# A two-layer attention and mixture-of-experts kernel: start-up order, clearing of the experts' buffer, where the padding of an expert's tiles lies, and the unit at which small work is done

## The reference, cut to what matters

```python
# x: (64, 64, 256), context: (64, 64, 256), float32
x = x + L0_xattn(layernorm(x), ctx)   # 8 heads of 8 channels, rotary, out projection
x = x + L0_ffn(layernorm(x))          # 64 experts, top 8 of a softmax, no capacity limit
x = x + L1_xattn(layernorm(x), ctx)   # 8 heads of 8, no rotary, no out projection
x = x + L1_ffn(layernorm(x))          # 64 experts, top 8, at most 128 rows for each expert
# attention: q, k, v projections (C = 64 channels, T = 256 positions, per batch),
#            softmax(q k / sqrt(8)) v
# expert:    (silu(x Wg) * (x Wu)) Wd, Wg and Wu 256 x 96, Wd 96 x 256, weighted and summed
```

## Time and profile before

| what | us |
|---|---|
| median of three runs | 2247.05 |
| the three runs | 2241.72 to 2247.66 |
| the profiled execution | 2246.79 |
| its span, first to last instruction | 2245.0 |

### The profile page before, as it was taken

How to read it: one execution, slowest core, us unless ns; L and a number is a source line. 1 busy time by engine, 2 the same in 40 slices (tenths; PEclk the granted TensorE clock), 3 DMA queues, 4 the chain that set the end, 5 groups by cost and what they waited for, 6 DMA issues and landing times. The chain is left out here.

```text
span 2245.0 us, 45332 instructions
## 1 busy us (share of the span) xinstructions
PE 1681.1 (75%) x12724; PEld 1129.2 (50%) x12879; DVE 1462.2 (65%) x4525; ACT 1329.7 (59%) x3396; POOL 985.9 (44%) x1111
## 2 busy tenths in 40 slices
PE   1688888889882797999998177777777778756551
PEld 0355555555541686888987034444444444444431
DVE  3588888888863343555533378888889888853331
ACT  0377777777770454666665368777787878642110
POOL 1236666666666000000000665555556554128883
PEclk9799999999995898999999589999999999978996
DMA  4766767667647986666565676676667666338856
GB/s 150 206 179 180 185 180 186 185 182 190 178 129 218 311 275 204 184 189 186 183 192 176 171 190 175 171 170 172 169 171 173 169 168 164 93 114 200 186 103 109
DMA packets 420684, 399.24 MB, mean 178 GB/s; under 512 B 46171, under 2 KB 392667, under 8 KB 420443
## 3 DMA queue, kind: packets, MB, share of 16 engines
q1 hardware_dynamic: 345163, 264.16, 43.6%
q0 software_dynamic: 37904, 90.22, 16.3%
q10 hardware_dynamic: 37376, 41.96, 6.4%
HBM read 242.00 MB, written 178.42 MB: 187 GB/s over the span
## 5 line engine op out<-in xcount | busy, mean ns | idle before, releaser
L1009 DVE TENSOR_REDUCE mx<-psS 128x2 f32<-128x512 f32 x1024 | 691.1, 682 | 152.9 <-PE psS L1376 128.1
L818 ACT ACTIVATE prob<-psE 128x512 f32<-128x512 f32 x1024 | 598.2, 600 | 253.3 <-PE psE L1387 244.9
L702 POOL DMA_INDIRECT yg<-y_d,posb x256 | 265.0, 1035 | 764.8 <-DVE posb L1051 511.9
L1387 PE MATMUL psE<-q,k 128*128 128x256 bf16 x2048 | 396.6, 276 | 36.7 <-DMA q<-mlo 14.2
L1376 PE MATMUL psS<-k,q 128*128 128x512 bf16 x869 | 337.7, 391 | 60.2 <-DMA k<-k_stack_d 48.1
L1492 PE MATMUL psE<-wt,xgT 128*128 (+1 forms) x1536 | 327.6, 337 | 3.0 <-ACT xgT L910 2.6
L1328 DVE TENSOR_TENSOR hid<-sil,psE 128x96 f32<-128x96 f32 x384 | 97.4, 254 | 356.8 <-ACT sil L915 356.8
L690 POOL DMA_INDIRECT xs_d<-xr,posi x256 | 251.3, 982 | 105.9 <-ACT prob L818 66.3
L910 ACT COPY xgT<-psS 128x256 f32<-128x256 f32 x384 | 144.5, 376 | 228.8 <-PE psS L1486 209.3
L1403 PE MATMUL psO<-prob,v 128*32 128x256 f32 x4096 | 276.6, 388 | 0.8 <-ACT osb L799 0.8
L1387 PEld LDWEIGHTS psE<-q,k 128*128 128x128 bf16 x2048 | 189.9, 99 | 166.1 <-ACT prob L818 34.9
(11 more groups left out here) (212 smaller groups left out, 2630.5 us busy)
## 6 DMA issues: line engine op xcount, KB each, us to landing
xg<-xs_d SPq DMA_DIRECT2D x320, 128.0 KB, 2.5
y_d<-y_all SPq DMA_DIRECT2D x320, 128.0 KB, 2.1
q<-q_stack_d SPq DMA_DIRECT2D x128, 256.0 KB
k<-k_stack_d SPq DMA_DIRECT2D x128, 256.0 KB
wt<-in_gu ACTq DMA_DIRECT2D x128, 192.0 KB, 3.8
wt<-in_dn ACTq DMA_DIRECT2D x128, 96.0 KB, 4.4
q_stack_d<-parts SPq DMA_DIRECT2D x64, 192.0 KB
k_stack_d<-parts SPq DMA_DIRECT2D x64, 192.0 KB
```

What stands on the lines that cost most here:

```text
L702: g.indirect_dma_start(yg[:, k, :], None, y0_d[:, :], bass.IndirectOffsetOnAxis(posb[b][:, k:k + 1], 0)).then_inc(d_yg, 16)
L818: a.activation(prob[gr][:, u % 4, :], psE[ring][:, :], ACT.Exp, scale=SCALE).then_inc(s_exp, 1)
L1009: v_.tensor_reduce(mx[b][:, bg // 4, :].rearrange("p (h r) -> p h r", h=2)[:, :, (bg % 4) * 2 + tt], psS[(UNITS * (st.s0 - LAG["smax"]) + ...
L1387: ins = m_.matmul(psE[ring][:, i * T:(i + 1) * T], k2[b][:, bg, hh * T + i * P:hh * T + (i + 1) * P], q2[b][:, bg, :], start=True, stop=True)
```

## The change

1. Start. SP asks for the first rows of x and of the context before the tables; the tables sin and bias_c are issued by ACT; `k2` is zeroed by POOL and no longer by DVE; the pads and zero rows are written after the barrier; the waits for them move to their first use (DVE's first rotate, SP's first stack read).
2. The early weights are loaded at steps 9 to 14 (`AHEAD`) in both layers.
3. Clearing: the last 128 rows of each region in 64 transfers of 128 KB, two a step in steps 4 to 35. The padding of an expert now lies in front of its first tile, in the cleared rows of the region before; only expert 0 keeps it behind. So one clearing is left at the end of layer 0 attention. `odd_d` is cleared in 33 transfers, one every seventh job from 64 on.
4. The gathers of layer 1 are allowed at units 1, 2, 3, 5, 6, 7, 9 and 10, and the last two stand ahead of POOL's split work.
5. SP issues the stack writes ahead of the rows with the maximum.
6. Small work is moved by a unit, and `MISC` is reordered: mT1 to unit 1, RK to unit 2, mT0 to unit 9, and with them the work of ACT and DVE that reads or feeds them.

```diff
-CLEARS = 8
+CLEARS = E
+CLEAR_AT = 4
+AHEAD = 9
-ENDS = (16, 16, 32)
+ODD_EVERY = 7
-PACE = (0, 2, 4, 6, 8, 10, 12, 14)
+PACE = ((0, 2, 4, 6, 8, 10, 12, 14), (1, 2, 3, 5, 6, 7, 9, 10))
-    layer: [("RK", "place"), ("mT1", "attn"), ("V", "smax"), ("K", "front"), ("OT0", "back"), ("OT1", "back"),
-            ("Q", "front"), ("NT", "back"), ("XT", "route"), ("mT0", "smax"), last, ("LG", "route")]
+    layer: [("mT1", "attn"), ("RK", "place"), ("V", "smax"), ("K", "front"), ("OT0", "back"), ("OT1", "back"),
+            ("Q", "front"), ("NT", "back"), ("mT0", "smax"), ("XT", "route"), last, ("LG", "route")]
...
-        def clear_ends(eng, engine, half):
+        def clear_end(eng, engine):
             eng.wait_ge(s_guard, 1)
             eng.wait_ge(d_zero, 16 * CLEARS)
-            for first in range(half * FB, E, 2 * FB):
-                _, ends = nc.values_load_multi_w_load_instructions(
...
-                for end in ends:
-                    eng.dma_start(xs_d[bass.ds(end, P), :], xn_d[TOKENS:TOKENS + P, 0:T])\
-                       .then_inc(d_ends[group_of(first)], 16)
+            eng.dma_start(xs_d[bass.ds(ends[0], P), :], xn_d[TOKENS:TOKENS + P, 0:T]).then_inc(d_small, 16)
...
-                if job == ZERO_ODD:
-                    sp.dma_start(odd_d.rearrange("(n p) t -> n p t", p=P),
-                                 xn_d[TOKENS:TOKENS + P, 0:T].unsqueeze(0).broadcast_to((PAIRS + 1, P, T)))\
+                if job >= ZERO_ODD and (job - ZERO_ODD) % ODD_EVERY == 0 and (job - ZERO_ODD) // ODD_EVERY <= PAIRS:
+                    sp.dma_start(odd_d[row((job - ZERO_ODD) // ODD_EVERY), :], xn_d[TOKENS:TOKENS + P, 0:T])\
                       .then_inc(d_zero, 16)
... (SP before the barrier)
-            by_channel(cos, tables[0])
-            by_channel(sin, tables[1])
-            by_channel(bias_c, wts["bias"])
-            sp.wait_ge(s_pad, 2)
...
-            sp.wait_ge(d_setup, 16 * (2 + 2 * NB))
-            sp.wait_ge(d_table, 16 * 3 * HC)
+            load_x(Step(0, LAG["load"]))
+            load_ctx(Step(0, LAG["comb"]))
+            by_channel(sp, cos, tables[0])
+            barrier(sp, 1)
... (SP's step)
-                if L == 0 and 0 < st.s0 <= CLEARS:
-                    part = E // CLEARS
-                    first = (st.s0 - 1) * part
-                    sp.dma_start(xs_d.rearrange("(e r) t -> e r t", r=STRIDE)[first:first + part, LAST:STRIDE, :],
-                                 zeros.unsqueeze(0).broadcast_to((part, P, T))).then_inc(d_zero, 16)
+                if L == 0 and 0 <= st.s0 - CLEAR_AT < PAIRS:
+                    for e in (2 * (st.s0 - CLEAR_AT), 2 * (st.s0 - CLEAR_AT) + 1):
+                        sp.dma_start(xs_d[bass.ds(e * STRIDE + LAST, P), :], zeros).then_inc(d_zero, 16)
... (POOL)
+            for b in range(NB):
+                g.memset(k2[b][:, :, :].bitcast(F32), 0.0)
             barrier(pool, 1)
...
-                for k in (4, 5):
-                    moved(k, PACE[k])
+                for k in (4, 5) if L == 0 else (4, 5, 6, 7):
+                    moved(k, PACE[L][k])
... (ACT)
+            by_channel(act, sin, tables[1])
+            by_channel(act, bias_c, wts["bias"])
             barrier(act, 1)
-                    if u == 15 and st.s0 < EARLY // 2:
+                    if u == 15 and 0 <= st.s0 - AHEAD < EARLY // 2:
-                    if L == 1 and u == 2 and st.on("post"):
+                    if L == 1 and u == 3 and st.on("post"):
                         a.mul(hote[:, 1, :, :], hote[:, 0, :, :], part1[:, 0:1]).then_inc(s_hote, 1)
-                    if L == 0 and u == 9 and st.on("back"):
+                    if L == 0 and u == 8 and st.on("back"):
                         a.activation(nt[:, :], psM[item_bank(0, "NT")][:, 0:T], ACT.Identity,
-                    if u == 2 and st.on("attn"):
+                    if u == 1 and st.on("attn"):
                         max_rows("attn", 1)
-                    if u == 11 and st.on("route"):
+                    if u == 10 and st.on("route"):
                         a.copy(xT[:, :, :].rearrange("p c t -> p (c t)"), psM[item_bank(L, "XT")][:, 0:2 * P]).then_inc(s_xT, 1)
-                    if u == 11 and st.on("smax"):
+                    if u == 9 and st.on("smax"):
                         max_rows("smax", 0)
... (DVE)
-                    if u == 2 and st.on("place"):          # place, total
+                    if u == 3 and st.on("place"):
-                    if u == 0 and st.on("post") and L == 1:  # hote
+                    if u == 1 and st.on("post") and L == 1:
-                    if u == 3 and st.on("place"):          # then den, inv, weights: each a unit later
+                    if u == 4 and st.on("place"):
-                    if L == 0 and u == 5 and st.on("front"):
+                    if L == 0 and u == 4 and st.on("front"):
                         rotate(1)
-                    if L == 1 and u == 9 and st.on("back"):  # x1, the sum with the residual
+                    if L == 1 and u == 8 and st.on("back"):
-                    if u == 1 and st.on("post") and L == 1:  # hotr
+                    if u == 4 and st.on("post") and L == 1:
-                    if u == 3 and st.on("attn"):
+                    if u == 2 and st.on("attn"):
                         split_max("attn", 1)
-                    if u == 11 and st.on("smax"):
+                    if u == 10 and st.on("smax"):
                         split_max("smax", 0)
...
+                link(v_.scalar_tensor_tensor(cnt[:, 6, :], cnt[:, 2, :], float(P), cnt[:, 0, :], ALU.mult, ALU.subtract))
+                link(v_.memset(cnt[:, 6, 0:1], 0.0))
```

More of the change, by code:

```diff
@@ L554, in _, with load_x @@
-            sp.wait_ge(s_pool_set, 1)
-            sp.dma_start(xn_d[TOKENS:TOKENS + P, :], zf[:, :]).then_inc(d_setup, 16)
-            sp.dma_start(out[TOKENS:TOKENS + P, :], zf[:, 0:T]).then_inc(d_setup, 16)
-            sp.wait_ge(d_setup, 16 * (2 + 2 * NB))
-            sp.wait_ge(d_table, 16 * 3 * HC)
-            zeros = xn_d[TOKENS:TOKENS + P, 0:T]
-            barrier(sp, 1)
+            def load_x(st):
+                b, t = st.buf("load"), st.pair("load")
+                hold(sp, s_xn, last(st, "load", back=NB))
+                sp.dma_start(xin[b][:, :], (x, x1_d)[st.L][row(t), :]).then_inc(d_x[b], 16)
@@ L562, in body @@
             def body(st):
                 L = st.L
[L564 to L567, removed]
-                if L == 0 and 0 < st.s0 <= CLEARS:
-                    part = E // CLEARS
-                    first = (st.s0 - 1) * part
-                    sp.dma_start(xs_d.rearrange("(e r) t -> e r t", r=STRIDE)[first:first + part, LAST:STRIDE, :],
-                                 zeros.unsqueeze(0).broadcast_to((part, P, T))).then_inc(d_zero, 16)
+                first = L == 0 and st.s0 == 0
@@ L573, in body @@
+                if st.on("load") and not first:
+                    load_x(st)
+                if first:
+                    set_up()
                 if st.on("attn"):
@@ L583, in body @@
                     sp.dma_start(xn_d[row(t), :], xr[b][:, :]).then_inc(d_xn[b], 16)
[L584 to L588, removed]
-                                     part[:, :]).then_inc(d_max[1][b], 16)
                 if st.on("stack"):
@@ L599, in body @@
                               .then_inc(d_parts[b], 16)
-                if st.on("comb"):
-                    b, t = st.buf("comb"), st.pair("comb")
-                    hold(sp, s_vp, last(st, "comb", back=NB))
-                    sp.dma_start(ctx_t[b][:, :], ctx[row(t), :]).then_inc(d_ctx[b], 16)
+                if st.on("attn"):
+                    b = st.buf("attn")
+                    for i, (part, made) in enumerate(((mhi[1], s_mhi[1]), (mlo[1], s_mlo[1]))):
+                        sp.wait_ge(made, st.n("attn"))
+                        sp.dma_start(q2[b][MAXROW + i:MAXROW + i + 65:64, 4:8, :].rearrange("p g t -> p (g t)"),
+                                     part[:, :]).then_inc(d_max[1][b], 16)
+                if st.on("comb") and (L == 1 or st.s0 > LAG["comb"]):
+                    load_ctx(st)
                 if st.on("stack"):
@@ L837, in body @@
                         o_out("back", 3)
+                    if L == 0 and u == 8 and st.on("back"):
+                        act.wait_ge(s_ntp, st.n("back"))
+                        wait(act, s_wo, last(st, "back"))
+                        a.activation(nt[:, :], psM[item_bank(0, "NT")][:, 0:T], ACT.Identity,
+                                     bias=bias[:, 7:8]).then_inc(s_nt, 1)
                     if u == 8:
@@ L897, in body @@
                             a.activation(ex[:, :], logit[:, :], ACT.Exp, bias=ntop[:, 0:1]).then_inc(s_ex, 1)
-                    if L == 0 and u == 9 and st.on("back"):
-                        act.wait_ge(s_ntp, st.n("back"))
-                        wait(act, s_wo, last(st, "back"))
```

(9 more changed lines are left out.)

141 lines of the change are left out of this document (73 added, 68 removed).

## The result

The changed kernel takes 2178.19 us (median of 4 runs, 2177.73 to 2180.07), the kernel before on the same chip 2244.39 (4 runs, 2239.94 to 2247.66): ratio 0.9708, 95% interval 0.9687 to 0.9729. That is 66 us less, where the forecast had 145.5, and it lies outside the range of 2065 to 2155. The profiled execution of after has a span of 2176.2 us, 68.8 less than the one before.

A forecast was written before the change was run, and what follows sets the result against it. No engine was taken as always busy: both attention phases run near, not at, an engine's limit, and joints stand nearly idle. Terms 35 + (43 - 5) + 10 + 17.5 + 6 + 39 = 145.5 off 2246.8 give 2101 us, range 2065 to 2155.

The forecast's parts named there:

- start: Kernel start: earlier barrier, x and context loaded before it, earlier first stack write; 35 us gained (25 to 43).
- layer 0 attention with weights: Layer 0 attention: shorter steps gain 43 us over 28 steps, less 5 for weights in steps 9 to 14.
- to the experts: Way from layer 0 attention to the experts: earlier barrier 8 us, shorter weight wait 2; 10 us (7 to 13).
- odd_d: Middle of the layer 0 experts: PE's 15.09 us wait goes, following tiles speed up; 17.5 us (15 to 18).
- head of layer 1: First steps of layer 1: POOL's period falls from 16.3 to 15 us over four steps; 6 us (0 to 12).
- layer 1 attention: Layer 1 attention: step falls from 21.91 to 20.2 us as waits go; 39 us after weights (10 to 65).
- The layer 0 step: Layer 0 attention: waits for nt, rotate and stack reads go, step falls from 18.73 to 17.2 us.
- Behind weights: Steps 9 to 14: weight transfers cost 0.8 us a step over 6 steps, 5 us in each layer (0 to 11).
- The landing of the last scatter: End of layer 0 attention: landing about 3 us on a free queue; the sign was barrier within 4 us of last scatter.
- half given back: Rival: removed waits hide others in both layers, steps 18.0 and 21.1 us, 44 us less gain, 2145 us; chance 0.25.
- Slower: Rival: late gathers hold ACT at unit 1 of layer 1, delaying mlo1 and V; 2260 us; chance 0.03.
- late gathers: Rival: layer 1's early gathers slip and land no sooner, 1.2 us a step or 29 us back; 2130 us; chance 0.10.

The follow-up runs named there:

- the version with three slots: Changed kernel with DVE's last two layer 1 additions made one reduction over three slots, residual loaded by SyncE: 2159.23 us, later 2112.83 (0.9392).
- the last set: Fourth set of runs: three slots, it with edit 4 undone, it with large clearings, kernel before with the reduction; kernel before takes 2249 us beside it.
- three reorderings of GpSimd's work: Changed kernel with edit 4 undone, with old order but new units, and with rem ahead of gathers 6 and 7: 2222.11, 2223.36, 2228.61 us.
- two more around the reduction: Three-slot version with DVE's sums a unit earlier, then with rem ahead of gathers 6 and 7 as well: 2169.98 and 2179.89 us, against 2159.23.
- the variant with the old gathers: Changed kernel with edit 4 undone, layer 1 gathers in the old order and at the old units: 2222.11 us, ratio 0.9791.
- With rem first: Changed kernel with rem moved ahead of gathers 6 and 7 in layer 1, gather units kept: 2228.61 us, step 23.46.
- the variant with nine slots: Changed kernel with layer 1's four two-input additions made two reductions over nine slots, residual loaded by SyncE: 2233.38 us, ratio 0.9853.
- second and third set: Sets with the changed kernel rerun beside its variants: 2237.82 us (0.9885) in the second, 2227.98 (0.9822) in the third.
- first set: Four variants of the changed kernel: three reorderings of GpSimd's work and one with one-input additions; 2180.72 to 2228.61 us, kernel before 2271.
- the fourth: Set with the three-slot version and variants, the same as the last set: three slots 2112.83 us, kernel before 2248.86.
- The last kernel: Three-slot version with layer 0's clearings as eight transfers of 1,024 KB at steps 4 to 11: 2129.37 us, ratio 0.9458.

## Why the forecast was wrong

By its own steps, all read from the two profiled executions of the first comparison:

| step | forecast | found | from |
|---|---|---|---|
| start | 35 | 35.6 | first result at 81.76 against 117.35; first stack write at 25.66 |
| layer 0 attention with weights | 38 | 36.0 | pair 29: 71.6 us ahead |
| to the experts | 10 | 7.2 | first product at 661.90 against 740.71: 78.8 ahead |
| odd_d | 17.5 | 16.3 | first result transfer of layer 1 at 1153.6 against 1248.7: 95.1 ahead |
| head of layer 1 | 6 | 0.3 | result of pair 0: 95.3 ahead |
| layer 1 attention | 39 | -25.8 | result of pair 31: 69.5 ahead |

The failed step is "I take the new step at 20.2 ... 39 us". 65 of the 77 us of the miss stand there. Its reading of the waits was right: they went, all of them. What it took for granted was that DVE's 19.0 us a step would stay. It went to 20.8 (536.0/597 x 23.17), because two instructions that nobody touched came to stand beside two of POOL that edit 4 had moved. DVE was then at 90% of the step, and PE waited for its maxima, 2.5 us a step. Without the meeting the forecast's step nearly holds: 20.6 us is the common step of the version with three slots, in the last set. That its 2112.83 us is within 12 us of the 2101 forecast says little more, since it is another kernel.

The layer 0 step was right in mechanism and size: the waits for nt, rope and the stack reads are gone, PE is the bound, 17.5 us against 17.2. Behind weights six steps take 18.0, so 3 us and not 5. The landing of the last scatter took 6.5 us to the barrier (646.39 to 652.88), not 4, and PE waited 9.0 us for weights behind it. At the head of layer 1 POOL's first periods fell from 16.3, 16.5 and 16.8 us to 15.4, 15.9 and 16.3, not to 15: a gather beside VectorE's large addition took up to 2.02 us there. That brought the lead from 95.1 to 97.4 us, and it was lost again by the first result (95.3), in steps where the two additions were already beside rem and parts; the version with three slots keeps it (first result at 1246.16, not 1248.44). At the start the forecast had POOL's memsets stand behind DVE's, by the rule on two-port modes. No row bears that out: DVE's three memsets of 1024 elements take 0.91 us each beside POOL's, as in the kernel before. What POOL's memsets did hold up is a cast of DVE, 1.91 us instead of 0.22, until 0.1 us after their end at 8.51:

```profile
3.17 5.34 POOL L678 MEMSET k<- 128x2048 f32 x3 [0.15 <-issue]
```

```profile
3.89 0.91 DVE L983 MEMSET v<- 128x1024 f32 x1 [0.16 <-issue]
...
6.69 1.91 DVE L997 CAST iota_r<-iota_i 128x128 bf16<-128x128 int32 x1
```

So DVE's last copy ended at 12.5 us and not at 11.7; the barrier came there, as forecast, and the slip cost the forecast nothing. In the sum for the start the stack write's gain is 24.8 us, not 24.5.

Of the rivals, "half given back" had the size nearest to the result and the wrong place: it put the loss into both layers, and layer 0 lost none. "Slower" named ACT's wait for the gathers at unit 1, which did not come. The late gathers came nearest in kind: they had POOL held up by DVE. That happens too, to one gather a step (2.09 us instead of 0.95), and makes rem late, but where the meeting is gone it costs nothing. What costs is that DVE is held up by POOL. The forecast drew on the Trainium skill for two-port modes only and set it beside the memsets and the gathers. The same page of the Trainium skill (SBUF — State Buffer, "Who interferes with whom") has a second case: a VectorE instruction with two inputs in SBUF contends with a GpSimd instruction that reads SBUF, and a reduction never does. The trace agrees in both halves: 1490 and 1312 ns beside rem and parts instead of 403, and 1014 for the reduction beside the same rem. This second case is the one that decided. What would have shown it ahead is in the trace of before: rem's end 0.03 us ahead of the addition, with GpSimd's order about to be changed.

## What to carry to other kernels

Before work is moved on VectorE or GpSimd, lay both timelines side by side and ask what each two-input operation of the one meets on the other after the move; a margin of 0.03 us is no margin. An engine's busy time a step is not a constant of the code: when a wait vanishes and the step does not shrink, compare the mean durations of unchanged instructions first. Where a meeting can't be scheduled away, change the form of the operation: one reduction in place of two small additions took 69 us off here, while three reorderings of GpSimd's work left the step at 23.2 to 23.5 us, and two more around the reduction gained nothing.

## What the hardware showed that was not expected

- The recorded starts don't tell which of the two waits. In the kernel before the 512 addition starts 0.32 us ahead of rem (1620.96 and 1621.28), keeps its 0.68 us, and rem takes 0.2 more. In the variant with the old gathers it starts as far ahead (1625.47 and 1625.79), and it is the addition that takes 2.04 us, until 0.55 after rem's end, while rem keeps its 1.17. With rem first an addition that starts 0.35 us ahead of parts (1609.94 and 1610.29) takes 1.79 us. A held addition ends 0.28 us (256 elements) or 0.55 us (512) after POOL's instruction.
- A gather of POOL is held up by DVE's large two-input addition: 2.09 us beside it (from 1607.47, the addition from 1607.53 to 1608.73), 0.95 without; beside a reduction, which has one input, it took 0.95 (1615.35, the reduction from 1615.47, in the variant with nine slots). The gather reads its rows' numbers from SBUF; that this is the reason is argued, not shown.
- Reductions over rows 1 KB apart: 1.33 ns an element with two rows (682 ns for 512), 1.32 with three (1014 for 768), 1.86 with nine (2137 for 1152). Why nine rows are slower was not tried.
- The same code does not give back the same on every occasion. In the second and third set layer 0 of the changed kernel runs at 18.7 and 18.6 us a step instead of 17.6, and the gain shrinks from 2.9% to 1.2 and 1.8%. In the first set its variants have 18.8 to 18.9, in the fourth 17.7, and these two sets bear the same chip's number, so it is not shown to be a property of the chip. PE's waits of 260 to 540 us, in the changed kernel of the first comparison and then of the second set:

```profile
PE psM L1436 <- DVE nrm L1046: 6.6, 15, 0.4
PE psE L1405 <- issue: 3.8, 24, 0.2
```

```profile
PE psM L1437 <- ACT xn L875: 14.3, 10, 1.7
PE psM L1437 <- DVE mlo L1032: 4.4, 15, 0.3
```

  PE waits 1.4 us for xn in ten steps of fifteen, because ACT's exponentials ahead of it start late, with nothing in the profile that they would wait for. What delays them stays open. The last kernel was to tell whether the small clearings are the cause; in its set layer 0 ran at 17.7 us a step even with them, so it does not say.
